# A Mamba-2 mixer on one core: tokens of the second batch transposed by DMA

## The reference

```python
proj = xn @ in_proj_w.T                      # gate, hBC, dt
hBC = silu(conv4(hBC) + conv_b)              # hs, B, C
dt = softplus(dt + dt_bias)
X = hs * dt                                  # per chunk of 128 tokens
A_cs = cumsum(-exp(A_log) * dt)
Y_diag = ((C @ B.T) * exp(segsum(A_dt))) @ X
states = (B * exp(A_cs[-1] - A_cs)).T @ X    # carried over 4 chunks
Y_off = (C @ prev_states) * exp(A_cs)
y = Y_diag + Y_off + D * hs
xg = y * silu(gate)                          # then RMS norm per group of 1024
out = (normed * norm_weight) @ out_proj_w.T
x = x + out + ffn(xn)
```

## Time and profile before

| | |
|---|---|
| median of 3 runs | 1618.43 |
| the profiled execution | 1617.07, its span 1615.3 |
| PE busy | 1598.4 (99%) |
| PEld, DVE | 1342.4 (83%), 1390.4 (86%) |
| ACT, POOL | 1266.0 (78%), 1168.7 (72%) |
| DMA | 212 MB, mean 131 GB/s |

### The profile page before, as it was taken

The page is one execution under the profiler, slowest core; times in us unless marked ns, Lnnn a source line. Parts: engine busy times, 40 slices in busy tenths (PEclk is TensorE's granted clock), DMA queues, the critical chain, the costliest instruction groups (busy, mean ns, idle before and its releaser), DMA issues. The chain is left out here.

```text
span 1615.3 us, 29072 instructions
## 1 busy us (share of the span) xinstructions
PE 1598.4 (99%) x9668; PEld 1342.4 (83%) x9668; DVE 1390.4 (86%) x2356; ACT 1266.0 (78%) x2496; POOL 1168.7 (72%) x1496
## 2 busy tenths in 40 slices
PE   8999999999999999999999999999999999999998
PEld 7888888888888888888878888888888888888887
DVE  6988888888888888898889888888888988888887
ACT  3678888888888888878846888888888888888885
POOL 5548777778687776878774587777777768777685
PEclk9999999999999999999999999999999999999999
DMA  5244443444434445344314444444454444434431
GB/s 174 92 150 128 136 143 122 149 129 134 148 118 149 133 130 150 119 146 130 119 51 144 133 131 147 122 145 131 133 150 123 141 134 129 151 126 138 143 120 63
DMA packets 82372, 212.18 MB, mean 131 GB/s; under 512 B 11184, under 2 KB 27568, under 8 KB 81968
## 3 DMA queue, kind: packets, MB, share of 16 engines
q1 hardware_dynamic: 82224, 210.33, 41.7%
HBM read 207.14 MB, written 3.15 MB: 130 GB/s over the span
## 5 line engine op out<-in xcount | busy, mean ns | idle before, releaser
L653 POOL TENSOR_TENSOR xl<-xg,xh 128x256 fp32r<-128x256 f32 x254 | 290.7, 1166 | 319.4 <-ACT xh L482 318.8
L558 POOL TENSOR_TENSOR wl<-raw,wh 128x256 fp32r<-128x256 f32 x584 | 425.4, 758 | 76.6 <-ACT wh L325 76.6
L353 ACT ACTIVATE mt<-cs_row,cs_tok 128x128 f32<-128x128 f32 x1024 | 324.8, 391 | 0.0
L667 POOL TENSOR_TENSOR wol<-raw_o,woh 128x256 fp32r<-128x256 f32 x256 | 181.5, 729 | 30.5 <-ACT woh L472 30.5
L1223 DVE TENSOR_TENSOR mt<-mt,gt 128x1024 f32<-128x1024 f32 x128 | 200.7, 1568 | 0.0
L660 POOL TENSOR_TENSOR sqa<-sqa,sq 128x256 f32<-128x256 f32 x222 | 158.9, 735 | 0.8 <-ACT sq L499 0.8
L482 ACT ACTIVATE xh<-xg 128x512 fp32r<-128x512 f32 x128 | 81.0, 633 | 95.4 <-DVE xg L1203 95.4
L325 ACT ACTIVATE wh<-raw 128x1024 fp32r<-128x1024 f32 (+1 forms) x146 | 152.1, 1042 | 0.8 <-DMA raw<-in_w_dtag 0.8
L1000 DVE SCALAR_TENSOR_TENSOR cv<-bt,par_sb,cv 128x511 f32<-128x511 f32 (+2 forms) x192 | 142.9, 744 | 6.8 <-ACT cv L329 2.3
L1000 DVE SCALAR_TENSOR_TENSOR cv<-bh,par_sb,cv 128x511 f32<-128x511 f32 (+2 forms) x192 | 142.9, 744 | 4.5
L717 PE MATMUL bg<-xTh,wh 128*128 128x512 f32 x544 | 145.8, 390 | 0.0
(11 more groups left out here) (218 smaller groups left out, 3601.7 us busy)
## 6 DMA issues: line engine op xcount, KB each, us to landing
raw<-in_w_step SPq DMA_DIRECT2D x128, 512.0 KB, 3.5
cs_row<-cs_rows SPq DMA_DIRECT2D x128, 512.0 KB, 5.5
raw_o<-in_w_out SPq DMA_DIRECT2D x128, 256.0 KB, 4.1
ec_row<-ec_rows SPq DMA_DIRECT2D x256, 96.0 KB, 4.7
raw<-in_w_bc SPq DMA_DIRECT2D x16, 512.0 KB, 3.6
acc<-in_x SPq DMA_DIRECT2D x8, 256.0 KB, 5.3
cs_row<-in_w_ffn SPq DMA_DIRECT2D x2, 1024.0 KB, 6.6
out_dram<-acc SPq DMA_DIRECT2D x1, 1024.0 KB, 6.2
```

The source lines that it names most:

```text
L353: e = act.activation(mt[:, m % 2, h, chunk(j)], cs_row[:, m % 2, h, chunk(j)], ACT.Relu, bias=cs_tok[:, j, 2 * m + h:2 * m + h + 1], scale ...
L558: e = pool.tensor_tensor(wl[:, n % 2, cols], raw[:, n % 2, cols], wh[:, n % 2, cols].bitcast(F32), ALU.subtract)
L653: e = pool.tensor_tensor(xl[:, u, cols], xg[:, u, cols], xh[:, u, cols].bitcast(F32), ALU.subtract)
L667: e = pool.tensor_tensor(wol[:, 1 - u, cols], raw_o[:, 1 - u, cols], woh[:, 1 - u, cols].bitcast(F32), ALU.subtract)
```

## The change

It concerns mainly the second batch (b = 1), and there the steps 0 to 62.

- The PE's four transposes of h2 are left out in these steps. ACT copies h2 as 16-bit words into tg's buffer, low halves first and then high halves (`halves`); SP issues one transposing DMA of 128 x 1024 16-bit words into a new tile `turned`; POOL puts the halves together again in xt by two copies; DVE's `take_tokens` reads xt in place of the PSUM bank, writes xd, and writes xt in place. It stands behind the taps. Before ACT writes tg again it waits for the DMA's landing.
- The low parts wl of the 64 weight blocks are stored to memory in batch 0 (`keep_low`) and loaded from there in batch 1 (`load_low`); POOL's `split_lo` is left out in batch 1. The wait of the raw load is then on ACT's split.
- In batch 1 POOL multiplies the mask of the second head in every step (before its xl), and DVE that of the first alone.
- ACT splits the weights of step m+2 before it copies the state of chunk 0 (m > 1), and its drain at group ends comes behind the last tap.
- Small prologue tiles (ag, sc, ...) now lie inside `turned`.
- Before xt is written DVE waits for its own xd, in both batches.

```diff
+TURN_FROM = 1
+        turned = sb("turned", [P, 2 * NJ, P], U16)
+        halves = tg[:, :].bitcast(U16)
...
+        def by_dma(b, m):
+            return b >= TURN_FROM and 0 <= m < STEPS - 1
...
         def load(n):
-                sp.wait_ge(p_wl, did(n - 2))
+                b, m = step_of(n - 2)
+                if b == 1 and m >= 0:
+                    sp.wait_ge(a_wh, did(n - 2))
+                else:
+                    sp.wait_ge(p_wl, did(n - 2))
...
+            def keep_low(m):
+                sp.wait_ge(p_wl, did(step(0, m)))
+                sp.dma_start(low_parts[m], wl[:, step(0, m) % 2, :].bitcast(F32)).then_inc(st_low[m % 2], 16)
+            def load_low(m):
+                if m < 2:
+                    sp.wait_ge(t_c, did(GROUPS + (GROUPS - 2 + m)))
+                else:
+                    sp.wait_ge(t_g, did(STEPS + m - 2))
+                sp.wait_ge(st_low[m % 2], landed(m))
+                sp.dma_start(wl[:, step(1, m) % 2, :].bitcast(F32), low_parts[m]).then_inc(ld_low[m % 2], 16)
...
                 for m in range(-2, STEPS):
+                    if by_dma(b, m - 1):
+                        q = turn(b, m - 1)
+                        sp.wait_ge(a_half, did(q))
+                        sp.wait_ge(p_tok, did(q - 1))
+                        sp.dma_start_transpose(turned[:, :, :], halves).then_inc(ld_turn[q % 2], 16)
                     if m + 2 < STEPS or b + 1 < NB:
                         load(step(b, m + 2))
+                    if b == 0 and has(m):
+                        keep_low(m)
+                    if b == 1 and has(m + 1):
+                        load_low(m + 1)
...
ACT  act.activation(woh[:, 1 - u, :], raw_o[:, 1 - u, :], ACT.Copy).then_inc(a_woh, 1)
+                        if early_split:
+                            act.wait_ge(t_g, did(n))
+                            split_hi(step(b, m + 2))
                         if m > 1:
                             first_state()
...
+                        if by_dma(b, m - 1):
+                            act.wait_ge(ld_turn[turn(b, m - 1) % 2], landed(turn(b, m - 1)))
                         act.activation(tg[:, :], bg[:, :], ACT.Tanh, scale=0.5).then_inc(a_tg, 1)
...
+                    if by_dma(b, m):
+                        act.wait_ge(v_h2, did(un))
+                        act.wait_ge(v_sg, did(n))
+                        act.activation(halves.rearrange("p (two t) -> p two t", two=2),
+                                       h2[:, u, :].bitcast(U16).rearrange("p (t two) -> p two t", two=2),
+                                       ACT.Copy).then_inc(a_half, 1)
                     if has(m):
                         rises(b, m, 1)
...
POOL
-                    if m == STEPS and b + 1 == NB:
+                    if has(m - 1) and b + 1 == NB:
...
+                    if by_dma(b, m - 1):
+                        q = turn(b, m - 1)
+                        pool.wait_ge(ld_turn[q % 2], landed(q))
+                        pool.wait_ge(t_d, did(n - 2))
+                        to = xt[:, :, :].bitcast(U16).rearrange("p j (c two) -> p two j c", two=2)
+                        for half in range(2):
+                            e = pool.tensor_copy(to[:, half], turned[:, NJ * half:NJ * (half + 1), :])
+                        e.then_inc(p_tok, 1)
...
-                    if m >= -1 and (has(m + 1) or (m < STEPS + 1 and b + 1 < NB)):
+                    if m >= -1 and b == 0 and (has(m + 1) or (m < STEPS + 1 and b + 1 < NB)):
                         split_lo(step(b, m + 1))
...
PE
-                    if has(m):
+                    if has(m) and not by_dma(b, m):
                         pe.wait_ge(v_h2, did(un))
                         for j in range(NJ):
                             mm = pe.transpose(mine[:, chunk(j)], h2[:, u, chunk(j)], ident[:, :])
...
DVE
+                        if by_dma(b, m - 1):
+                            dve.wait_ge(p_tok, did(turn(b, m - 1)))
+                            x_d, x_t = xt[:, 0:NS, :], xt[:, :, :]
...
-                    if has(m - 1) and not ahead:
+                    if has(m - 1) and not ahead and not by_dma(b, m - 1):
                         take_tokens()
...
-                        mask_decays()
+                        mask_decays(2 if b + 1 < NB else 1)
...
                         for k in range(1, TAPS):
                             tap(n, un, u, mine, k)
+                        if by_dma(b, m - 1):
+                            take_tokens()
```

More of the change, by code:

```diff
@@ L168, in mixer_kernel @@
         v_pick, v_some = sem("v_pick"), sem("v_some")
+        st_low, ld_low = [sem(f"st_low{i}") for i in range(2)], [sem(f"ld_low{i}") for i in range(2)]
+        a_half, p_tok, ld_turn = sem("a_half"), sem("p_tok"), [sem(f"ld_turn{i}") for i in range(2)]
         a_dr, p_acc, t_fin, v_xl = sem("a_dr"), sem("p_acc"), sem("t_fin"), sem("v_xl")
@@ L200, in has, with turn, turned_by_pe, wait_turned @@
             return 0 <= m < STEPS
+        def by_dma(b, m):
+            return b >= TURN_FROM and 0 <= m < STEPS - 1
+        def turn(b, m):
+            return (b - TURN_FROM) * (STEPS - 1) + m
+        def turned_by_pe(b, m):
+            return b * STEPS + m if b < TURN_FROM else TURN_FROM * STEPS + b - TURN_FROM
+        def wait_turned(eng, b, m):
+            if m < 0:
+                b, m = b - 1, m + STEPS
+            if b >= 0:
+                if by_dma(b, m):
+                    eng.wait_ge(a_half, did(turn(b, m)))
+                else:
+                    eng.wait_ge(t_t, did(turned_by_pe(b, m)))
         def bank_y(b, m):
@@ L462, in first_state @@
                         act.activation(S[:, 0, :], other[:, 0:P], ACT.Copy).then_inc(a_s1, 1)
+                    early_split = m > 1 and by_dma(b, m) and (has(m + 2) or b + 1 < NB)
                     def weights_and_state():
@@ L482, in _ @@
                         act.activation(xh[:, u, :], xg[:, u, :], ACT.Copy).then_inc(a_xh, 1)
-                    if has(m - 2) and m > 2 and (m - 2) % PER_GROUP == 0:
+                    ended = has(m - 2) and m > 2 and (m - 2) % PER_GROUP == 0
+                    if ended and not by_dma(b, m):
                         drain((n - 2) // PER_GROUP - 1)
@@ L490, in _ @@
                         last_tap(un, u, mine)
+                        if ended and by_dma(b, m):
+                            drain((n - 2) // PER_GROUP - 1)
                         if m == 0:
@@ L520, in _ @@
                             take_b(b, GROUPS - 1)
-                    if has(m) and (has(m + 2) or b + 1 < NB):
+                    if has(m) and not early_split and (has(m + 2) or b + 1 < NB):
                         act.wait_ge(t_g, did(n))
@@ L556, in split_lo @@
                 pool.wait_ge(a_wh, did(n))
+                b, m = step_of(n - 2)
+                if b == 0 and m >= 0:
+                    pool.wait_ge(st_low[m % 2], landed(m))
                 for cols in pieces(width(n)):
@@ L714, in project @@
                     if i == 2:
-                        pe.wait_ge(p_wl, did(n))
+                        _, m = step_of(n)
+                        if b == 1 and m >= 0:
+                            pe.wait_ge(ld_low[m % 2], landed(m))
+                        else:
+                            pe.wait_ge(p_wl, did(n))
                     for k in range(KT):
@@ L1256, in conv_product @@
                         def conv_product():
[L1257 removed]
+                            wait_turned(dve, b, m - 2)
                             if m == 1:
```

45 lines of the change are left out of this document (24 added, 21 removed).

## The result

The changed kernel takes 1621.68 us (median of 10 runs, 1619.59 to 1623.01), the one before 1618.03 in the same series (10 runs, 1616.03 to 1618.59). The ratio is 1.0022, 95% interval 1.0012 to 1.0032: slightly slower, where 1603.3 was forecast. The profiled execution took 1622.38, with a span of 1620.7 against 1615.3.

The account below looks back on a forecast made before the run. TensorE's list was taken to bound each step; transposes -31.5, state reads +6, xl +3, group ends +5, start +2.4 sum to -15.1: 1602.0 profiled, 1603.3 median, forecast's own range 1595 to 1612, wide range 1587 to 1640.

Parts of the forecast that it names:

- plain step: Second batch's ordinary step on TensorE: 11.14 before, 10.64 without the transposes, expected at 10.7 to 10.9 with losses.
- state reads: TensorE's reads of S at a step's end: VectorE's last update slightly late, 0.1 lost in 61 steps, 6 us.
- transposing DMA: From the halves to its landing: 4.1 taken (3 to 6), no loss up to 4.3.
- group ends: ScalarE's drain of 1.83 in 7 steps, with 0.35 idle left as cover: 0.7 each, 5 us (0 to 10).
- steady loss: Loss per step to the other engines: 0.1 for the state reads (6 us) and 0.05 for xl (3 us).
- xl's late arrival: GpSimd's xl behind mask and copies, with xd between its halves: 0.05 a step, 3 us (0 to 90).
- The start: Second batch's beginning: the states' input comes at 902.7, wanted at 900.25, a stall of 2.4 us, once.
- my chain: At the batch's start: halves 1.0, DMA 4.1, copies 1.4, xd and xt 1.2, gate's product 0.7, ending at 902.7.
- transposes: Four transposes off TensorE's list, 0.50 a step, 63 times: 31.5 us, the most the change can give.
- wide range of 1587 to 1640: Time from the packed case, TensorE without gaps, up into the late DMA; about 0.02 below and 0.12 above.
- late DMA: Rival, chance 0.21: landing from 4.8 after issue makes the step longer than 11.14; 1659 us at 5.5.
- GpSimd's order: Rival, chance 0.14: mask, copies and collisions ahead of xl make the loop 11.0 to 11.2; time 1612 to 1622.

Follow-up runs that it names:

- thin drain: Changed kernel with ScalarE's drain of the output banks at group ends cut from 512 to 8 columns per block: 1613.86 us, ratio 0.9977.
- TensorE's turning of step 0: Changed kernel with TensorE turning step 0 and steps m mod 8 = 0, weights' split behind the exponentials, drain behind the last tap: 1609.22 us, ratio 0.9947.
- thin sum: Changed kernel with GpSimd's running sum of squares cut to 4 columns in the second batch: 1614.27 us, ratio 0.9979.
- late split alone: Changed kernel with only ScalarE's split of the weights put back behind the exponentials in all steps: 1618.73 us, ratio 1.0005.
- version with the lowest median: Changed kernel with TensorE turning step 0 and steps m mod 8 = 0, 1, 2, and the split behind the exponentials: 1606.41 us, ratio 0.9934.

## Why the prediction was wrong

**What stood.** L954 (now L1041) falls by 252, from 512 to 260. The plain step is 10.86, within 10.7 to 10.9. The state reads lose 0.11 where 0.1 was forecast: ScalarE's copy of the state starts 9.25 into the step (9.2 forecast) and VectorE's updates end at 10.54 (10.5). The early split has no part in it, as the run without it showed; the path from the states over the copy to the updates has lost the 0.5 of cover. The halves take 1.05 (1.0), GpSimd's copies 1.46 the pair (1.4), its mask 1.89 (1.9). The loads, the stores and the low part cost nothing, as the run without the turning showed. The transposing DMA comes in time: over the steady stretch GpSimd waits for it once, 0.4. The halves end at 1209.68, SP's issue starts at 1209.70 and the copies start at 1213.85 without a wait, so it takes at most 4.2 there. The Trainium skill's Advanced Engine Details and Errata (X-Bar Transpose) says that such a DMA is as fast as a plain one, and the trace agrees: the plain load of the same size takes 5.0. The Trainium skill's VectorE: DVE Perf Modes (The three transpose paths) has 1309 ns for one block; adding that up over eight blocks, 10.5 us, does not agree with the trace.

**The step that failed: group ends.** I charged 0.7 seven times, 5 us, for ScalarE's drain. Measured is 12.55 + 11.98 - 2 x 10.86 - 0.48 (the 0.48 by which a group end was longer before) = 2.33 seven times, 16.3 us. Of this the drain and the early split make the second step's 1.12 (1.18 by the run with the thin drain), and 0.7 was too low even for that. The other 1.21 is in the first step and is VectorE's list, which I did not charge at all. I had checked VectorE in a plain step, with 1.38 idle, but not in the one where the squares' 1.38 come on top, after xd and xt had moved ahead of the states and grown to 1.98 together. Two runs remove one half each: the thin drain the second step's, and TensorE's turning of step 0, with which VectorE's products are early and short, the first step's.

Against the 1602.0 forecast for a profiled execution, which took 1622.38, the group ends are 11.3 of the 20.4 us missed.

**The steady loss.** I charged 0.05 a step for xl's late arrival. xl is on time; in its place the states are late by 0.11, because xt meets GpSimd's sum of squares. The prediction had xd and xt collide, but charged it on xl alone. The whole loss is 0.22 a step, not 0.15, and 13.6 us instead of 9 over 62 steps. The running sum's two halves take 2.21 and xt 1.04 when they meet, 0.69 alone; the Trainium skill's SBUF — State Buffer (Who interferes with whom) has this exclusion, and the trace agrees.

**The start.** The stall was forecast at 2.4 and is 3.8, and the first states are 4.1 late. Turning the first step on TensorE removes it, as that run showed. The trace shows the pieces that my chain lacked. GpSimd's copies start at 900.61, behind its mask (to 900.67) and without a wait for the DMA, and end at 902.03, 0.5 later than in my chain; and VectorE takes the tokens behind its taps, which had waited 1.30 for ScalarE and end at 902.98, 0.9 later still:

```profile
900.67 2.31 DVE L1087 SCALAR_TENSOR_TENSOR cv<-bt,par_sb,cv 128x511 f32<-128x511 f32 x3 [1.30 <-ACT cv L385]
```

The slow clock behind the stall is in the batch's first step: 12.42, which is 1.56 above a plain one where 0.98 was usual, 0.6 more. Turned by TensorE the batch starts at the full clock, but that step is then 12.55, with a wait of 0.9 for sg.

**The end** was not in the sum. Of its 1.6 some 0.2 are waits (for xt 1.11 where it was 0.92), and 1.5 are the clock (below): the last twelve matmuls take 4.50 from first start to last end, 3.02 before, up to 0.63 each instead of 0.40. That part does not seem to be in every execution: of the ten of the kernel after, the four with a mean granted clock of 0.998 or 0.999 took 1619.59 to 1620.75, the six with 0.996 or 0.997, the profiled one among them, 1621.65 to 1623.01.

**Sum by the prediction's terms**, forecast and measured: transposes -31.5 and -31.0 (62 intervals); steady loss 9 and 13.6; group ends 5 and 16.3; start 2.4 and 4.1; end 0 and 1.6. With the 0.6 of the first step that makes 5.2; the span says 5.4. The measured time lies inside the wide range of 1587 to 1640, but its part above 1612 was there for a late DMA and for GpSimd's order, and neither came about. (The chances of a faster kernel add up to 0.68 and not 0.67, those of no change to 0.09.) No rival had this place. The nearest, GpSimd's order, gave 1612 to 1622, but neither of its signs (GpSimd never waiting, xl late over 0.5 in each step) is there: GpSimd waits 103.5 for the exponentials, and xl is not late.

## What to carry to other kernels

Work that is taken off the bounding engine was also the time in which the others handed in. Before it is removed, sum each other engine's list not for the plain step but for the longest one (the drain, the reduction, the first of a batch), and keep the old way in just those steps: here the change is worth 0.66% with it and costs 0.22% without. When an order of instructions hangs on a flag that also chooses the algorithm, a run that changes the flag tests both.

## What the runs showed of the hardware

After the stall of 3.78 at the start of the batch the granted clock was 0.87, 0.50 (1.2 GHz) and 0.78 in three windows of 2 us; the sixteen L1031 matmuls took 1.75 there and 1.09 elsewhere. All four traces with this stall have such a fall behind it (the kernel after, the thin drain, the thin sum, the late split alone), and none of the other nine has one at that place. So a stall of the bounding engine can cost its own length and some more.

At the end the clock of the kernel after was 0.51 and 0.64 from 1612 to 1616. What brought it down is open: the PE had been busy for 5.54 of the 7 us from 1599 and 5.48 of the 6 from 1606, and in the kernel before, busy for 5.54 of 7 us from 1595 and 5.46 of 6 from 1602, it stayed at 1.00 to its last matmul. Eight of the eleven traces of experiments have such a fall at the end.

In the profiled run of the version with the lowest median one step took 14.62 (1453.47 to 1468.09). VectorE's mask and then GpSimd's instructions beside it, ahead of that step:

```profile
1448.54 4.04 DVE L1318 TENSOR_TENSOR mt<-mt,gt 128x512 f32<-128x512 f32 x1
```

```profile
1447.81 1.43 POOL L719 TENSOR_TENSOR mt<-mt,gt 128x256 f32<-128x256 f32 x2
1449.20 1.43 POOL L737 TENSOR_TENSOR xl<-xg,xh 128x256 fp32r<-128x256 f32 x2
1450.59 1.43 POOL L744 TENSOR_TENSOR sqa<-sqa,sq 128x256 f32<-128x256 f32 x2
```

VectorE's mask, 1.16 in the median, took 4.04: it ended at 1452.58, after an unbroken row of GpSimd's instructions had ended at 1452.02, while each of GpSimd's pairs took its 1.43. The Trainium skill's SBUF — State Buffer (Who interferes with whom) has one instruction block the other for its whole length; here, once in 62, VectorE's seems to have been blocked through five (inferred from the times). The PE then waited 1.73 for S, and the clock was 0.79 for 8 us. That version's runs took 1605.5 to 1606.4 three times, at a mean clock of 0.999 or 1.0, and 1611.2 and 1612.1 (the profiled one) at 0.997; whether the other of these two had such a step is open, as only one run has a trace.

SP is held for 1.24 us by the issue of one transposing DMA of 256 KB in a plain step, against 0.38 to 0.58 for a plain load. SP's issues in that step end at 1214.45 and the next is at 1220.57, so here it had the room.
